# The squared deviations of four subsets: summed on GpSimd, and one averaging product behind the even image's first product

## The chip, the cores and the metric

The kernel runs on one core of a Trainium2 chip. The metric is the device time of the whole kernel in microseconds (us). Several engines work side by side: TensorE (PE) multiplies matrices, VectorE (DVE), ScalarE (ACT) and GpSimd (POOL) work elementwise, and 16 DMA engines move data between memory and the core's SBUF. SyncE (SP) only issues transfers here. The engines meet at semaphores.

## The reference, cut to what matters

```python
x = x + conv_block(group_norm(x, groups=32))          # x: (32, 512, 28, 28) float32

# group_norm: (x - mean) / sqrt(var + 1e-5) over 16 channels x 784 pixels of an image
# conv_block(v):
xg = v.reshape(B, 4, 128, H, W)[:, [1, 2, 3, 0]]      # groups rotated by one
xa = round(clip((xg - lA) / (uA - lA), 0, 1) * 15) / 15
wq = (round(clip((weight - lW) / (uW - lW), 0, 1) * 15) / 15 - 0.5) * 2
y  = einsum('bgihw,goi->bgohw', xa, wq.reshape(4, 128, 128))
y  = relu(y * inv + (beta - running_mean * inv))      # inv = gamma / sqrt(running_var + 1e-5)
return y + v
```

An image has 512 channels x 784 pixels in float32, 1.606 MB (1568 KB). All 32 are read once and written once.

## The kernel before, in words

**Tiling.** An image is four groups of 128 channels (one channel a partition) by 784 pixels. Images stand in a ring of `RING` = 12 buffers in SBUF. SyncE's queue loads image n whole; from n = 12 on it first waits until image n - 12 has been stored from the same buffer. ScalarE's queue stores images 0 to 29 whole, each once VectorE has finished its four groups; image 30 (L203) and the four groups of image 31, one by one (L212), are stored from SyncE's queue.

**Statistics, two images (a pair u) at a time.** For groups 0 and 1 VectorE takes means and squared deviations of four subsets of each channel's pixels (L460) and sums them over the subsets (`sum_stats`, L468); for groups 2 and 3 ScalarE takes the channel's mean (L236) and squared deviations from it (L242). Pairs 0 and 1 have three groups on VectorE. TensorE averages over the 16 channels of a norm group with a constant matrix: `average_means` gives the group means (L575, L576) and the first part of the variance (L578, which begins the sum in `var_ps`). ScalarE copies the means to SBUF (`gmean`, L250). GpSimd's `deviations` subtracts them from the subset means (L375) or channel means (L378), 2 images x 4 groups x 4 subsets, and squares the 32 values a channel (L382). `average_deviations` (L584) adds them to `var_ps` with one product for each of the four subsets. The variance then goes on: ScalarE makes half the variance and the standard deviation (L256, L257), VectorE the reciprocal (`rough_rstd`, L492), GpSimd a Newton step and the coefficients of two affine maps (`coefficients`, L398 to L406, each link waiting for the one before).

**The work on an image.** ScalarE (L270) and, for one group, GpSimd (L424) turn the input into levels; VectorE caps all four groups at once to bf16 codes (`cap`, L475). TensorE multiplies them by the weight, which is split in three bf16 parts: six matmuls of 392 columns a group (`multiply`, L604). Meanwhile GpSimd writes the affine part x + normalised x over the input (`affine`, L413; for the last four images ScalarE takes two of the groups, L278). TensorE waits for that affine before the last matmul of a group's product, so that VectorE's `finish` (L482), which adds the larger of product and floor to the image, needs only one semaphore.

**Order.** Each engine runs a list written out by hand. In round n GpSimd runs the affines of image n + 1 and its part of the levels of n + 2; before an odd n + 1 it makes the coefficients of the next pair, and in an even n + 1, behind the first affine, the `deviations` of pair (n + 3) // 2. VectorE runs finish 0 and 1 of image n, the cap of image n + 1, finish 2 and 3, the statistics of image n + 5 between and behind them, and for odd n the reciprocal at the end of the round. ScalarE runs levels, the stores, the sums of image n + 5, `deviation` (half variance and standard deviation) and the squares. TensorE runs the four products of image n + 1; for odd n `average_deviations` stands in front of the first, for even n `average_means` in front of the fourth. Three product buffers in PSUM (`SETS` = 3) stand between TensorE and VectorE. For pairs 0 and 1 the averages stand before and behind the very first product, an order of its own.

Of the kernel before, what the change touches and what calls it, by code (L numbers as in the profile page):

```python
# [5 lines left out]
ALU = mybir.AluOpType  # L6
ACT = mybir.ActivationFunctionType
AXIS = mybir.AxisListType
F32 = mybir.dt.float32
# [3 lines left out]
P = 128  # L13
# [13 lines left out]
SUBSETS = 4  # L27
# [3 lines left out]
def fused_norm_quantised_conv(nc, x, weight, limits, channel_params, out):  # L31

    B, C, H, W = x.shape
    G = CONV_GROUPS
# [11 lines left out]
    def stats_on_dve(u):  # L46
        return 3 if u < 2 else 2
# [6 lines left out]
    def affine_on_act(n):  # L54
        return 2 if n >= B - HELPED else 0
# [13 lines left out]
    def squares_until(u):  # L69
        return sum(2 * (G - stats_on_dve(i)) for i in range(u + 1))  # L70
# [7 lines left out]
    def output_group(g):  # L78
        return (g + G - 1) % G

    with ExitStack() as ctx:
        def sb(name, shape, dtype):
            return ctx.enter_context(nc.sbuf_tensor(name, shape, dtype))

        def ps(name, shape, dtype):
            return ctx.enter_context(nc.psum_tensor(name, shape, dtype))

        def sem(name):
            return ctx.enter_context(nc.semaphore(name))
# [8 lines left out]
        unused = sb("unused", [P, 2, HW], BF16)  # L98
        gmean = sb("gmean", [P, 2, 2, G], F32)
        dev = sb("dev", [P, 2, G, SUBSETS], F32)  # L100
        dev2 = sb("dev2", [P, 2, G, SUBSETS], F32)
        half_var = sb("half_var", [P, 2 * G], F32)
        std = sb("std", [P, 2, G], F32)
        rough = sb("rough", [P, 2, G], F32)
# [26 lines left out]
        avg = sb("avg", [P, P], F32)  # L131
# [5 lines left out]
        var_ps = ps("var_ps", [P, 512], F32)  # L137
# [26 lines left out]
        dev_step = sem("dev_step")  # L164
        dev_done = sem("dev_done")
        var_done = sem("var_done")
# [162 lines left out]
        def _(pool):  # L329
            step = [0]  # L330

            def chained(ins):
# [33 lines left out]
                                    cols[:, 1].unsqueeze(1).to_broadcast([P, 2, G]),  # L366
                                    bn[:, 4].unsqueeze(1).to_broadcast([P, 2, G]), ALU.subtract)

            def deviations(u):
                k, par = stats_on_dve(u), u % 2  # L370
                pool.wait_ge(gmean_done, u + 1)
                if u >= 1:
                    pool.wait_ge(var_done, u)
                mean = gmean[:, par].unsqueeze(3)
                nc.gpsimd.tensor_tensor(dev[:, :, 0:k], stats[:, par, :, 0:k, :, 1],  # L375
                                        mean[:, :, 0:k].to_broadcast([P, 2, k, SUBSETS]), ALU.subtract)
                own = sums[:, par, 0].unsqueeze(3)
                nc.gpsimd.tensor_tensor(dev[:, :, k:G], own[:, :, k:G].to_broadcast([P, 2, G - k, SUBSETS]),  # L378
                                        mean[:, :, k:G].to_broadcast([P, 2, G - k, SUBSETS]),
                                        ALU.subtract).then_inc(dev_step, 1)  # L380
                pool.wait_ge(dev_step, u + 1)
                nc.gpsimd.tensor_tensor(dev2[:], dev[:], dev[:], ALU.mult).then_inc(dev_done, 1)  # L382

            LINKS = 6

# [172 lines left out]
        @block.tensor  # L558
        def _(pe):
            pe.wait_ge(consts_done, 1)  # L560
            pe.wait_ge(rows_in, DMA)
            nc.tensor.transpose(cols_ps[:, 0:4 * G], rows[:], ident[0:4 * G, 0:4 * G])
            pe.wait_ge(limits_in, DMA)
            nc.tensor.matmul(cols_ps[:, 4 * G:5 * G], one_row[:], limit_row[:], start=True,
                             stop=True).then_inc(cols_turned, 1)

            def average_means(u):
                k, par = stats_on_dve(u), u % 2
                pe.wait_ge(bn_summed, u + 1)
                pe.wait_ge(squared, squares_until(u))  # L570
                if u >= 1:
                    pe.wait_ge(gmean_done, u)
                    pe.wait_ge(std_done, u)
                mean = mean_ps[:, 0:2 * G].rearrange("p (j g) -> p j g", g=G)
                nc.tensor.matmul(mean[:, :, 0:k], avg[:], sums[:, par, 0, :, 0:k], start=True, stop=True)  # L575
                nc.tensor.matmul(mean[:, :, k:G], avg_one[:], sums[:, par, 0, :, k:G], start=True,  # L576
                                 stop=True).then_inc(mean_done, 1)
                nc.tensor.matmul(var_ps[:, 0:2 * G], avg_n[:], sums[:, par, 1], start=True, stop=False)  # L578

            def average_deviations(u):  # L580
                pe.wait_ge(dev_done, u + 1)
                var = var_ps[:, 0:2 * G].rearrange("p (j g) -> p j g", g=G)
                for s in range(SUBSETS):
                    done = nc.tensor.matmul(var, avg[:], dev2[:, :, :, s], start=False, stop=(s == SUBSETS - 1))  # L584
                done.then_inc(var_done, 1)


            def wait_affine(n, g):
                if g < G - affine_on_act(n):
                    pe.wait_ge(y_pool, (y_pool_until(n - 1) if n else 0) + g + 1)  # L590
                else:
                    pe.wait_ge(y_act, y_act_until(n - 1) + g - (G - affine_on_act(n)) + 1)

            def multiply(n, g):
                k = G * n + g
                if g == 0:
                    pe.wait_ge(capped, n + 1)
                if k >= SETS:
                    pe.wait_ge(final, k - SETS + 1)
                for part in range(PARTS):  # L600
                    for h in range(2):
                        if (part, h) == (PARTS - 1, 1):
                            wait_affine(n, g)
                        done = nc.tensor.matmul(prod[:, k % SETS, h, 0:HALF], w_t[:, part, output_group(g)],  # L604
                                                codes[:, n % 2, g, h * HALF:(h + 1) * HALF],
                                                start=(part == 0), stop=(part == PARTS - 1))
                done.then_inc(multiplied, 1)

            pe.wait_ge(w_scaled, 1)
            for g in range(G):  # L610
                turned = nc.tensor.transpose(prep_ps[:, g], w_raw[:, g], ident[:])
            turned.then_inc(w_turned, 1)
            average_means(0)
            average_deviations(0)
            pe.wait_ge(w_ready, 1)

            for n in range(-1, B - 1):
                if n < 0:
                    average_means(1)
                    multiply(0, 0)  # L620
                    average_deviations(1)
                    multiply(0, 1)
                    multiply(0, 2)
                else:
                    if n % 2 and (n + 3) // 2 < PAIRS:
                        average_deviations((n + 3) // 2)
                    multiply(n + 1, 0)
                    multiply(n + 1, 1)
                    multiply(n + 1, 2)
                    if n % 2 == 0 and (n + 4) // 2 < PAIRS:  # L630
                        average_means((n + 4) // 2)
                multiply(n + 1, 3)
# [23 lines left out]
```

## Time and profile before

| | before |
|---|---|
| median of 3 runs | 258.73 us (258.67 to 258.85) |
| profiled execution, its own time | 258.41 us |
| its span, first to last instruction | 256.7 us |
| mean granted TensorE clock | 0.902 of full speed |
| TensorE busy | 193.9 us (76%) |
| VectorE busy | 230.0 us (90%) |
| ScalarE busy | 215.2 us (84%) |
| GpSimd busy | 212.0 us (83%) |
| moved | 103.25 MB, mean 402 GB/s |

The profile is of one execution. "Span" leaves out what lies before the first and behind the last instruction, 1.7 us here. Busy shares are averages over the whole span; in the middle of it VectorE, ScalarE and GpSimd are each busy over nine tenths of the time. In the rows below a name such as L604 is a line of the kernel. "a<-b" is output and inputs, x6 the number of instructions merged in a row, and a bracket at the end the idle time in front of it with what ended it. The row of lengths of a merged group runs from its first start to its last end.

### The profile page before, as it was taken

What the parts mean: (1) busy time and instruction counts of PE and PEld (TensorE: products, weight loads), DVE (VectorE), ACT (ScalarE), POOL (GpSimd) and SP (SyncE); (2) the same over time, 40 slices, a digit from 0 to 9 for tenths busy, and PEclk for the clock granted to TensorE, in tenths of its full rate; (3) what the DMA queues carried; (4) which work ended last, traced back from release to release, by engine and by line L of the source; (5) the groups of instructions that cost most, each with busy time, mean ns of one, the idle gap of its engine ahead of it and who ended that gap; (6) DMA issues with size and microseconds to landing.
All of it is one profiled execution on the core that took longest, in us unless ns stands there. A gap on an engine that the chain in (4) does not pass through costs nothing.

```text
span 256.7 us, 3463 instructions
## 1 busy us (share of the span) xinstructions
PE 193.9 (76%) x999; PEld 109.3 (43%) x999; DVE 230.0 (90%) x363; ACT 215.2 (84%) x394; POOL 212.0 (83%) x340
## 2 busy tenths in 40 slices
PE   1142996969889888979797997877696969889920
PEld 0132644435454444445443554343444435454510
DVE  2898698999999999999999899999999999969940
ACT  4437898999999999989999889999899888999300
POOL 6126869999999999999999999999999999999100
PEclk9999999797979798988979599999979797979995
DMA  6999999999999999999999999999999999999994
GB/s 225 398 411 411 408 409 406 418 416 417 418 414 418 417 416 418 411 418 416 416 415 416 418 416 413 419 417 415 417 413 418 416 418 409 402 400 402 393 399 193
DMA packets 34516, 103.25 MB, mean 402 GB/s; under 512 B 1202, under 2 KB 1730, under 8 KB 34498
## 3 DMA queue, kind: packets, MB, share of 16 engines
q1 hardware_dynamic: 18624, 54.86, 53.8%
q10 hardware_dynamic: 15874, 48.18, 47.0%
q8 instruction: 8, 0.13, 0.2%
q14 instruction: 10, 0.08, 0.1%
HBM read 51.65 MB, written 51.38 MB: 401 GB/s over the span
## 4 chain that ended last, share of the span: by engine, by line
POOL 52%; DVE 16%; issue 11%; PE 9%; ACT 5%; DMA 2%; DVEq 0%; SPq 0%; POOLq 0%; ACTq 0%
POOL images L413 27%; POOL levels L424 8%; DVE images L482 7%; PE prod L604 6%; DVE stats L460 4%; POOL dev L375 3%; DVE codes L475 3%; PE var_ps L584 3%; POOL dev L378 2%; DMA images<-in_x 2%; POOL scaled L404 2%; ACT levels L270 2%; POOL coef L406 2%; POOL norm L402 1%; ACT unused L242 1%
## 5 line engine op out<-in xcount | busy, mean ns | idle before, releaser
L604 PE MATMUL prod<-codes,w_t 128*128 128x392 bf16 x768 | 160.8, 369 | 7.9 <-DVE codes L475 2.9
L482 DVE SCALAR_TENSOR_TENSOR images<-prod,floor,images 128x784 f32<-128x784 f32 x128 | 128.0, 1019 | 8.5 <-PE prod L604 8.2
L413 POOL TENSOR_SCALAR images<-images,coef 128x784 f32<-128x784 f32 x120 | 123.7, 1042 | 0.0
L604 PEld LDWEIGHTS prod<-codes,w_t 128*128 128x128 bf16 x768 | 79.1, 110 | 81.6 <-issue 24.6
L270 ACT ACTIVATE levels<-images,coef 128x784 int16<-128x784 f32 x95 | 91.3, 1028 | 1.1 <-issue 1.1
L460 DVE BATCH_NORM_STATS2 stats<-images 128x6 f32<-128x392 f32 x136 | 68.9, 551 | 5.4 <-DMA images<-in_x 5.4
L236 ACT ACTIVATE unused<-images 128x784 bf16<-128x784 f32 x60 | 50.7, 847 | 7.5 <-DMA images<-in_x 5.2
L242 ACT ACTIVATE unused<-images,sums 128x784 bf16<-128x784 f32 x60 | 56.1, 939 | 0.1
L475 DVE TENSOR_SCALAR codes<-levels 128x3136 bf16<-128x3136 int16 x32 | 34.7, 1085 | 1.0 <-ACT levels L270 0.7
L584 PE MATMUL var_ps<-dev,avg 128*128 128x8 f32 x128 | 19.6, 280 | 20.0 <-POOL dev L382 20.0
L424 POOL TENSOR_SCALAR levels<-images,coef 128x784 int16<-128x784 f32 x33 | 33.6, 1020 | 0.1
L584 PEld LDWEIGHTS var_ps<-dev,avg 128*128 128x128 f32 x128 | 18.6, 221 | 25.4 <-POOL dev L382 25.2
L375 POOL TENSOR_TENSOR dev<-stats,gmean 128x16 f32<-128x16 f32 (+1 forms) x16 | 10.9, 682 | 9.6 <-ACT gmean L250 9.6
L575 PE MATMUL mean_ps<-sums,avg 128*128 128x4 f32 (+1 forms) x32 | 6.5, 274 | 12.2 <-DVE sums L468 12.2
L575 PEld LDWEIGHTS mean_ps<-sums,avg 128*128 128x128 f32 x32 | 5.2, 203 | 17.2 <-DVE sums L468 12.2
L242 ACT ACTIVATION_READ_ACCUMULATOR unused<-images,sums 128x1 f32 x60 | 11.4, 190 | 0.0
L236 ACT ACTIVATION_READ_ACCUMULATOR unused<-images 128x1 f32 x60 | 11.3, 188 | 0.0
L256 ACT ACTIVATE half_var<-var_ps,eps 128x8 f32<-128x8 f32 x16 | 4.2, 265 | 6.7 <-PE var_ps L584 6.4
L398 POOL TENSOR_TENSOR newt<-rough 128x8 f32<-128x8 f32 x16 | 3.9, 242 | 5.5 <-DVE rough L492 5.5
L250 ACT ACTIVATE gmean<-mean_ps 128x8 f32<-128x8 f32 x16 | 2.7, 170 | 6.1 <-PE mean_ps L576 6.0
L278 ACT ACTIVATE images<-images,coef 128x784 f32<-128x784 f32 x8 | 7.7, 1032 | 0.0
L404 POOL TENSOR_TENSOR scaled<-norm,coef_mul 128x32 f32<-128x32 f32 x16 | 6.5, 409 | 1.2
(66 smaller groups left out, 83.2 us busy)
## 6 DMA issues: line engine op xcount, KB each, us to landing
images<-in_x SPq DMA_DIRECT2D x30, 1568.0 KB, 14.5
out<-images ACTq DMA_DIRECT2D x30, 1568.0 KB, 18.8
images<-in_x SPq DMA_DIRECT2D x8, 392.0 KB, 6.6
out<-images SPq DMA_DIRECT2D x1, 1568.0 KB, 8.8
out<-images SPq DMA_DIRECT2D x4, 392.0 KB, 7.4
w_raw<-in_weight SPq DMA_DIRECT2D x1, 256.0 KB, 6.5
rows<-in_channel_params ACTq DMA_DIRECT2D x1, 8.0 KB, 2.3
limit_row<-in_limits ACTq DMA_DIRECT2D x1, 0.0 KB
```

The source lines that it names most:

```text
L236: nc.scalar.activation(unused[:, g % 2], images[:, n % RING, g], ACT.Identity, scale=1.0 / HW, accum_out=sums[:, u % 2, 0, j, g:g + 1]).th ...
L242: nc.scalar.activation(unused[:, g % 2], images[:, n % RING, g], ACT.Square, scale=-1.0, bias=sums[:, u % 2, 0, j, g:g + 1], accum_out=sum ...
L270: nc.scalar.activation(levels[:, n % 2, g], images[:, n % RING, g], ACT.Relu, bias=coef[:, u % 2, 1, 0, G * j + g:G * j + g + 1], scale=co ...
L375: nc.gpsimd.tensor_tensor(dev[:, :, 0:k], stats[:, par, :, 0:k, :, 1], mean[:, :, 0:k].to_broadcast([P, 2, k, SUBSETS]), ALU.subtract)
L413: nc.gpsimd.tensor_scalar(here, here, coef[:, u % 2, 0, 1, G * j + o:G * j + o + 1], coef[:, u % 2, 1, 1, G * j + o:G * j + o + 1], ALU.mu ...
L424: nc.gpsimd.tensor_scalar(levels[:, n % 2, g], images[:, n % RING, g], coef[:, u % 2, 0, 0, G * j + g:G * j + g + 1], coef[:, u % 2, 1, 0, ...
L460: nc.vector.bn_stats(two, images[:, n % RING, g, h * HALF:(h + 1) * HALF]).then_inc(bn_done, 1)
L475: nc.vector.tensor_scalar(codes[:, n % 2], levels[:, n % 2], 0.0, TOP, ALU.max, ALU.min).then_inc(capped, 1)
L482: nc.vector.scalar_tensor_tensor(out=two, in0=prod[:, k % SETS, :, 0:HALF], scalar=floor[:, o:o + 1], in1=two, op0=ALU.max, op1=ALU.add).t ...
L575: nc.tensor.matmul(mean[:, :, 0:k], avg[:], sums[:, par, 0, :, 0:k], start=True, stop=True)
L584: done = nc.tensor.matmul(var, avg[:], dev2[:, :, :, s], start=False, stop=(s == SUBSETS - 1))
L604: done = nc.tensor.matmul(prod[:, k % SETS, h, 0:HALF], w_t[:, part, output_group(g)], codes[:, n % 2, g, h * HALF:(h + 1) * HALF], start= ...
```

## The change

GpSimd no longer stops at the 32 squares a channel. It adds the four subsets in two steps, 16 additions and then 8, so that 8 values (2 images x 4 groups) are left. Each of the two steps that read what the one before wrote waits for its semaphore. TensorE averages these 8 with one product instead of four. And in the rounds with odd n this product stands behind the first product of the even image n + 1 instead of in front of it. The order for pairs 0 and 1 stays.

```diff
-        dev2 = sb("dev2", [P, 2, G, SUBSETS], F32)
+        dev2 = sb("dev2", [P, 2 * G, SUBSETS], F32)
+        dev2_half = sb("dev2_half", [P, 2 * G, SUBSETS // 2], F32)
+        dev2_sum = sb("dev2_sum", [P, 2 * G], F32)
...
+            FOLDS = 3
+
+            def folded(u, k, ins):
+                ins.then_inc(dev_step, 1)
+                pool.wait_ge(dev_step, FOLDS * u + k)
+
             def deviations(u):
...
-                nc.gpsimd.tensor_tensor(dev[:, :, k:G], own[:, :, k:G].to_broadcast([P, 2, G - k, SUBSETS]),
-                                        mean[:, :, k:G].to_broadcast([P, 2, G - k, SUBSETS]),
-                                        ALU.subtract).then_inc(dev_step, 1)
-                pool.wait_ge(dev_step, u + 1)
-                nc.gpsimd.tensor_tensor(dev2[:], dev[:], dev[:], ALU.mult).then_inc(dev_done, 1)
+                folded(u, 1, nc.gpsimd.tensor_tensor(dev[:, :, k:G], own[:, :, k:G].to_broadcast([P, 2, G - k, SUBSETS]),
+                                                     mean[:, :, k:G].to_broadcast([P, 2, G - k, SUBSETS]), ALU.subtract))
+                dev_ = dev[:].rearrange("p j g s -> p (j g) s")
+                folded(u, 2, nc.gpsimd.tensor_tensor(dev2[:], dev_, dev_, ALU.mult))
+                folded(u, 3, nc.gpsimd.tensor_tensor(dev2_half[:], dev2[:, :, 0:2], dev2[:, :, 2:4], ALU.add))
+                nc.gpsimd.tensor_tensor(dev2_sum[:], dev2_half[:, :, 0], dev2_half[:, :, 1], ALU.add).then_inc(dev_done, 1)
...
             def average_deviations(u):
                 pe.wait_ge(dev_done, u + 1)
-                var = var_ps[:, 0:2 * G].rearrange("p (j g) -> p j g", g=G)
-                for s in range(SUBSETS):
-                    done = nc.tensor.matmul(var, avg[:], dev2[:, :, :, s], start=False, stop=(s == SUBSETS - 1))
-                done.then_inc(var_done, 1)
+                nc.tensor.matmul(var_ps[:, 0:2 * G], avg[:], dev2_sum[:], start=False, stop=True).then_inc(var_done, 1)
...
                 else:
+                    multiply(n + 1, 0)
                     if n % 2 and (n + 3) // 2 < PAIRS:
                         average_deviations((n + 3) // 2)
-                    multiply(n + 1, 0)
                     multiply(n + 1, 1)
```

## Rows read from the trace of the kernel before

**Rows 1.** The page: DMA share and GB/s in 40 slices; the chain by engine.
```profile
DMA  6999999999999999999999999999999999999994
...
GB/s 225 398 411 411 408 409 406 418 416 417 418 414 418 417 416 418 411 418 416 416 415 416 418 416 413 419 417 415 417 413 418 416 418 409 402 400 402 393 399 193
...
POOL 52%; DVE 16%; issue 11%; PE 9%; ACT 5%; DMA 2%; DVEq 0%; SPq 0%; POOLq 0%; ACTq 0%
```

**Rows 2.** Busy time by windows: window, length, engines, PEclk, DMA share, GB/s.
```profile
235.00:240.00 5.00, 4.50 (x28) 2.43 (x26) 5.00 (x6) 4.89 (x6) 3.48 (x3) 1.00 1.04 403
...
250.00:255.00 5.00, 0.00 (x0) 0.00 (x0) 0.00 (x0) 0.00 (x0) 0.00 (x0) 0.55 0.68 266
...
255.00:256.00 1.00, 0.00 (x0) 0.00 (x0) 0.00 (x0) 0.00 (x0) 0.00 (x0) 0.50 0.02 9
```

**Rows 3.** Timeline around the deviations of one pair: start, length, engine, line.
```profile
110.96 1.17 PE L604 MATMUL prod<-codes,w_t 128*128 128x392 bf16 x6
...
111.76 0.97 DVE L475 TENSOR_SCALAR codes<-levels 128x3136 bf16<-128x3136 int16 x1
...
111.82 0.99 POOL L378 TENSOR_TENSOR dev<-sums,gmean 128x16 f32<-128x16 f32 x1
...
112.89 0.24 POOL L382 TENSOR_TENSOR dev<-dev 128x32 f32<-128x32 f32 x1
...
113.11 2.96 POOL L413 TENSOR_SCALAR images<-images,coef 128x784 f32<-128x784 f32 x3
...
113.18 1.21 PE L584 MATMUL var_ps<-dev,avg 128*128 128x8 f32 x8 [1.05 <-POOL dev L382]
...
114.59 0.26 ACT L257 ACTIVATE std<-var_ps,eps 128x8 f32<-128x8 f32 x1
...
116.42 0.18 DVE L492 RECIPROCAL rough<-std 128x8 f32<-128x8 f32 x1
...
117.01 0.20 POOL L398 TENSOR_TENSOR newt<-rough 128x8 f32<-128x8 f32 x1
...
117.29 0.21 POOL L399 TENSOR_TENSOR newt<-newt,half_var 128x8 f32<-128x8 f32 x1
```

**Rows 4.** Timeline: the squarings of pairs 2 and 15.
```profile
43.42 0.24 POOL L382 TENSOR_TENSOR dev<-dev 128x32 f32<-128x32 f32 x1
...
225.04 0.24 POOL L382 TENSOR_TENSOR dev<-dev 128x32 f32<-128x32 f32 x1
```

**Rows 5.** Timeline of the end: VectorE and the issues of stores.
```profile
228.10 1.03 DVE L482 SCALAR_TENSOR_TENSOR images<-prod,floor,images 128x784 f32<-128x784 f32 x1 [1.01 <-PE prod L604]
...
230.06 1.03 DVE L482 SCALAR_TENSOR_TENSOR images<-prod,floor,images 128x784 f32<-128x784 f32 x1 [0.93 <-PE prod L604]
...
238.55 0.38 ACTq L262 DMA_DIRECT2D out<-images  x1
...
241.20 5.73 DVE L482 SCALAR_TENSOR_TENSOR images<-prod,floor,images 128x784 f32<-128x784 f32 x6
...
243.19 0.39 SPq L203 DMA_DIRECT2D out<-images  x1
```

**Rows 6.** Chain that ended last, in order of time: start, length, what.
```profile
0.79 0.38 SPq L191
...
1.70 5.61 DMA images<-in_x
```

**Rows 7.** Timeline of the start.
```profile
22.84 0.19 ACT L242 ACTIVATION_READ_ACCUMULATOR unused<-images,sums 128x1 f32 x1
...
26.86 2.14 PE L604 MATMUL prod<-codes,w_t 128*128 128x392 bf16 x6 [0.55 <-DVE codes L475]
...
28.79 1.71 PE L584 MATMUL var_ps<-dev,avg 128*128 128x8 f32 x8
...
30.54 0.27 ACT L256 ACTIVATE half_var<-var_ps,eps 128x8 f32<-128x8 f32 x1 [0.91 <-PE var_ps L584]
```

**Rows 8.** Who waited for whom: total us, times, longest.
```profile
POOL newt L398 <- DVE rough L492: 5.5, 3, 2.8
```

## The prediction, made before the kernel was changed

> **What bounds the kernel now.** I read the page's slices first. The DMA row stands at 9 from the second slice to the last but one [rows 1]: the 103 MB of loads and stores keep all 16 DMA engines occupied from about 5 us on, so that a compute engine that gets faster has nothing to give by itself. The GB/s row shows three stretches: about 410 while only loads run (to about 40 us), about 416 while loads and stores mix, about 401 when only stores are left (from about 215 us). The second look is at the last 20 us. At 235 to 240 us the engines are full at 403 GB/s; from 250 us on, 266 GB/s x 5 us = 1.33 MB are still moved, and the last traffic lies between 255 and 256 us [rows 2]. At 401 GB/s those 1.33 MB would be done at 253.3 us: this is the mean engine's end. The last of the 16 ends near 255.5 us. The difference, 2.2 us, is skew between the engines.
>
> The third view is the chain of waits: 52% of the chain that ended last is GpSimd [rows 1]. In the timeline of a pair of images GpSimd's instructions follow each other with no wait in front of them [rows 3], and the squaring of the deviations comes at 43.42 us for pair 2 and at 225.04 us for pair 15 [rows 4]: 181.6 us for 13 pairs, 13.97 us a pair. For a pair the DMA engines move four images of 1.606 MB (two in, two out), 15.4 us at 416 GB/s. So there are two clocks. Compute, paced by GpSimd, is the faster one by 1.5 us a pair, and the difference stands in a backlog of stores, until about 215 us. From there only stores are left, 4.0 us each at 401 GB/s, while compute delivers one each 7 us and at the end one each 4.65 us (238.55 and 243.19 us, [rows 5]): the backlog is eaten. When image 30's store is issued at 243.19 us, images 30 and 31 still need 2 x 1.606 / 0.401 = 8.0 us. The mean engine has 253.3 - 243.2 = 10.1 us to go, so its backlog ahead of them is 2.1 us; the last engine's is 255.5 - 243.2 - 8.0 = 4.3 us. A new store takes time before it moves data: the first load is issued at 0.79 and the transfer that the chain follows begins at 1.70 us [rows 6], 0.9 us. So compute may end later by 2.1 - 0.9 = 1.2 us before the mean engine runs dry ahead of image 30, and by 4.3 - 0.9 = 3.4 us before the last one does. That slack is what the change must be measured against.
>
> **The change part by part.**
>
> *Two adds more on GpSimd, in each of 16 pairs.* Now the squaring (0.24 us) is followed at once by the next affine, 113.11 - 112.89 = 0.22 us after its start [rows 3]. Afterwards: a link of the coefficients, 0.20 us of work, is followed by the next after 117.29 - 117.01 = 0.28 us, so its wait adds 0.08 [rows 3]. The squaring with such a wait is 0.24 + 0.08 = 0.32 us; the add of 16 elements with one 0.28 us (the link has 8); the last add, 0.20 us. Together 0.80, less 0.22: 0.58 us a pair. From below, an add could cost only its 0.20 us, 0.40 together; from above, L378 with 16 elements took 0.99 us where VectorE's 4x-rate cap of 3136 elements ran beside it (111.76 to 112.73 us, [rows 3]), some 0.77 us more than alone. But GpSimd, never idle, meets each of the two caps of a pair already; a third meeting would need a third cap. I take 0.58. Nothing hides it, since GpSimd waits for nobody: pairs 2 to 14 add 13 x 0.58 = 7.5 us by the time that pair 15 is reached. Behind the adds in GpSimd's queue stand three affines of the even image (TensorE's last matmul of each product waits for them), then its part of the quantising (the cap waits for it), then the next pair's coefficients.
>
> *Six TensorE instructions less a pair* (three fp32 matmuls, each seen twice, with their loads). The eight take 1.21 us in [rows 3], so some 0.9 us goes; with them goes the 1.05 us in which TensorE stood before the squares. TensorE is not what paces the pairs, so this is worth nothing in the steady state; it cancels part of the delay elsewhere.
>
> *The averaging product behind the first product.* The first product starts when its cap is done (112.73 us) and needs 1.17 us at the high clock, as that at 110.96 us, to about 113.95. The sum of squares is ready at 112.89 + 0.80 = 113.7. So the averaging product runs from about 113.95 to 114.35, where the eight instructions now end at 113.18 + 1.21 = 114.39 [rows 3]. The variance arrives when it did, though 0.58 us of it was added: ScalarE and VectorE see no new delay. At the low clock the product takes about 2.1 us (the first one, 26.86 us, [rows 7]) and the variance comes up to 0.9 us later; the standard deviation, done at 114.85 us, lies for 1.57 us before VectorE's reciprocal takes it at 116.42 us [rows 3], which covers it.
>
> *The start.* For pairs 0 and 1 the old order stays, and TensorE's burst is on the path. For pair 1 the eight take 1.71 us and ScalarE waits 0.91 us for them [rows 7]; GpSimd stands idle for the reciprocal behind the second product [rows 8]. Two instructions instead of eight give back 1.2 us there; the 0.58 us of GpSimd lies in its wait. For pair 0 ScalarE's own statistics end when the coefficients do, so only about 0.2 us comes through (22.84 us, [rows 7]). Gain: 1.4 us, once.
>
> *The few waits that GpSimd does have.* It waits for the reciprocal three times, 5.5 us in all, 2.8 us the longest [rows 8]; all but 0.3 us of that is in pairs 0 and 1. Another 0.2 us or so stands before the means. A later GpSimd doesn't wait: 0.5 us back.
>
> *The end.* In pair 15 TensorE sets the pace once: VectorE waits 1.01 and 0.93 us for products 0 and 1 of image 28 [rows 5], because the averaging stands in front of both. With product 0 ahead of it I give back 1.4 us of these 1.94 (between 0.9 and 1.9).
>
> *The sum.* Compute ends later by 7.5 - 1.4 - 0.5 - 1.4 = 4.2 us: VectorE's last write moves from 246.9 [rows 5] to 251.1, and image 30's store from 243.2 to 247.4. The slack for the last engine is 3.4 us: 0.8 us is left over. By the mean engine (slack 1.2) it would be 3.0. Since the end is that of the last of the 16, I go near the lower: +1.0 us. The profiled execution took 258.41 us, span 256.7; it becomes 259.4 with span 257.7. The median of the runs is 0.3 us above it: 258.73 + 1.0 = 259.7.
>
> The Trainium skill ("DMA: Bandwidth & Descriptors", on the anatomy of one DMA) puts a fixed cost of about 2 us on each DMA, most of it the receipt of the write. Such a receipt counts at the very end, where it stands now too, so that the sum is the same; were all 2 us in front of the data, the time would be 1.1 us above my figure. The trace shows 0.9 us in front at the first load and, behind the last traffic, about 1 us to the end of the span.
>
> **Rivals.**
>
> *Hidden.* The time stays within 258.2 to 259.2. This needs compute to end no more than 3.9 us later, for instance with adds at 0.5 us a pair (13 x 0.08 = 1.0 us less) or an end that gives back all 1.9. The DMA row at 9 throughout speaks for it; against it, the deliveries at the end have a margin that the sum uses up. Place of the forecast within this: 258.9.
>
> *Faster.* The 16 engines share what memory gives; if the ones that run dry leave their share to the slow ones, the skew of 2.2 us goes. Image 30's store then ends at 243.2 + d + 0.9 + 8.0 = 252.1 + d against 255.5, with d the delay of compute, but not before the mean's 253.3. It is faster by over 0.5 us for d under 2.9. With d = 2.4 this gives -1.0 us, 257.7. That d is under 2.9 needs GpSimd's addition to be 0.48 us a pair or less, and the skew has survived all of the run so far. Little speaks for it. The earlier first store (0.9 us at 416 instead of 410 GB/s) is worth 0.01 us.
>
> *Much slower.* GpSimd loses more than its two adds (a cap that fell across an affine and now holds two small ones, or VectorE held up by GpSimd's quantising, which it follows closely): 0.8 us a pair, d = 7.1, 3.7 us left over for the last engine: 262.4.
>
> **How the numbers follow.** What this kernel's runs can tell from no change is about 0.2%, 0.5 us. Forecast (slower by 0.5 to 3 us, likeliest 259.7): 0.57. Hidden: 0.28. Faster: 0.08. Much slower: 0.07. Slower is 0.57 + 0.07 = 0.64. The range takes in the hidden case down to 258.3 and goes up to the mean-engine bound, 258.73 + 3.0, cut a little: 261.5. It leaves out the faster and the much slower case and some of each edge, about 0.18.
>
> **What would show each step right or wrong.** The distance of the squarings of pairs 2 and 15, 181.6 us now, should be 189 us (187 to 190); if it stays under 184, the adds don't pace the pairs. The L413 behind the last add should begin 0.80 us after the squaring. The averaging should be two instructions a pair with no wait on GpSimd of more than 0.3 us, and end as early after the squaring as before. VectorE's last write should come at about 251 us, image 30's store at 247.4. The DMA row should show its first gap behind 235 us, where there is none now: 1 us windows below 0.9 between 238 and 250. If compute ends 4 us later and the span is the same, the skew gave it back; if compute doesn't end later, GpSimd wasn't the pace.

## The result, and the profile of the changed kernel

| | before | changed |
|---|---|---|
| median, 6 runs each | 258.70 us (258.44 to 258.93) | 259.88 us (259.35 to 260.25) |
| ratio | | 1.0041, 95% interval 1.0026 to 1.0057 |
| span of the profiled execution | 256.7 us | 257.8 us |
| TensorE busy | 193.9 us | 169.0 us |
| GpSimd busy | 212.0 us | 219.5 us |

The kernel became slower by 0.4%, 1.1 to 1.2 us; forecast was 259.7 us with a span of 257.7. TensorE is busy 25 us less and the kernel is later all the same. Of the 25 us, 13.0 are the averaging products (19.6 us before, 6.6 after) and 6.4 the image products, which are as many as before and run at a higher mean granted clock (0.947, before 0.902).

The page of the changed kernel, the same slices and chain as in [rows 1]:

```profile
DMA  6999999999999999999999999999999999998798
...
GB/s 214 396 411 411 409 406 414 415 418 416 418 418 414 418 416 418 416 412 417 418 417 418 414 417 417 417 419 413 414 418 418 417 413 411 402 389 332 315 363 324
...
POOL 70%; issue 9%; DVE 6%; DMA 6%; SPq 2%; ACT 2%; PE 2%; DVEq 0%; POOLq 0%; ACTq 0%
```

GpSimd's share of the chain rose from 52% to 70%. The GB/s row is nearly the old one as far as slice 35 and falls to 332 and 315 in slices 37 and 38, where the kernel before kept 402 and 393: the transfers run short of work near the end. In windows of 1 us (same columns as [rows 2]; the share of the DMA engines is the last number but one):

```profile
232.00:233.00 1.00, 1.00 (x6) 0.77 (x5) 0.32 (x1) 0.15 (x1) 1.00 (x2) 0.50 0.83 323
...
233.00:234.00 1.00, 1.00 (x5) 0.47 (x4) 0.69 (x2) 1.00 (x3) 0.86 (x3) 0.50 0.54 210
...
238.00:239.00 1.00, 1.00 (x8) 0.53 (x6) 1.00 (x2) 1.00 (x2) 1.00 (x2) 1.00 0.17 66
...
243.00:244.00 1.00, 1.00 (x8) 0.62 (x7) 1.00 (x2) 1.00 (x2) 1.00 (x2) 1.00 0.33 126
...
248.00:249.00 1.00, 1.00 (x8) 0.59 (x7) 1.00 (x2) 0.00 (x0) 0.00 (x0) 1.00 0.45 182
...
255.00:256.00 1.00, 0.00 (x0) 0.00 (x0) 0.00 (x0) 0.00 (x0) 0.00 (x0) 0.50 1.03 408
...
256.00:257.00 1.00, 0.00 (x0) 0.00 (x0) 0.00 (x0) 0.00 (x0) 0.00 (x0) 0.50 0.48 185
```

At 233 to 234 us the engines are 0.54 busy, at 238 to 239 only 0.17, at 243 to 244 0.33, at 248 to 249 0.45. Each gap lies in front of the data of one more image. The first clear one, at 232 to 234 us, is in front of image 27, whose store is issued at 232.86 us (before at 226.63). Behind the last gap they stay full until 256 us and stop within 1 us, whereas before the traffic ebbed away over 3 us:

```profile
252.00:253.00 1.00, 0.00 (x0) 0.00 (x0) 0.00 (x0) 0.00 (x0) 0.00 (x0) 0.50 0.79 304
253.00:254.00 1.00, 0.00 (x0) 0.00 (x0) 0.00 (x0) 0.00 (x0) 0.00 (x0) 0.50 0.43 166
254.00:255.00 1.00, 0.00 (x0) 0.00 (x0) 0.00 (x0) 0.00 (x0) 0.00 (x0) 0.50 0.14 53
```

One pair in the timeline, against [rows 3]:

```profile
111.84 0.99 POOL L422 TENSOR_SCALAR images<-images,coef 128x784 f32<-128x784 f32 x1
...
111.97 1.75 DVE L484 TENSOR_SCALAR codes<-levels 128x3136 bf16<-128x3136 int16 x1 [0.32 <-ACT levels L272]
...
113.77 1.17 PE L610 MATMUL prod<-codes,w_t 128*128 128x392 bf16 x6 [1.78 <-DVE codes L484]
...
114.05 0.24 POOL L389 TENSOR_TENSOR dev<-dev 128x32 f32<-128x32 f32 x1
...
114.36 0.21 POOL L390 TENSOR_TENSOR dev_half<-dev 128x16 f32<-128x16 f32 x1
...
114.66 0.20 POOL L391 TENSOR_TENSOR dev_sum<-dev_half 128x8 f32<-128x8 f32 x1
...
114.84 2.94 POOL L422 TENSOR_SCALAR images<-images,coef 128x784 f32<-128x784 f32 x3
...
114.91 0.39 PE L591 MATMUL var_ps<-dev_sum,avg 128*128 128x8 f32 x2
...
115.50 0.26 ACT L259 ACTIVATE std<-var_ps,eps 128x8 f32<-128x8 f32 x1
...
117.40 0.18 DVE L501 RECIPROCAL rough<-std 128x8 f32<-128x8 f32 x1
...
119.29 1.08 POOL L409 TENSOR_TENSOR newt<-three_halves,newt 128x8 f32<-128x8 f32 x1
...
119.34 0.96 DVE L484 TENSOR_SCALAR codes<-levels 128x3136 bf16<-128x3136 int16 x1
```

The affine behind the adds starts 0.79 us after the squaring (114.84 - 114.05), where it was 0.22. TensorE's first product (113.77) now stands in front of the averaging, which is two instructions of 0.39 us and is over at 115.30, 1.25 us behind the start of the squaring; it was 1.50 before. (Where the first product falls in a stretch of the low clock the averaging comes later. In the next pair the product takes 2.14 us at half the clock and ScalarE waits 1.67 us for the averaging; in all it waits 11.1 us, 6.4 before.) ScalarE's standard deviation is done at 115.76 and VectorE takes it at 117.40: 1.6 us of cover, as before.

The squarings of pairs 2 and 15, against [rows 4]:

```profile
41.07 0.24 POOL L389 TENSOR_TENSOR dev<-dev 128x32 f32<-128x32 f32 x1
...
230.77 0.24 POOL L389 TENSOR_TENSOR dev<-dev 128x32 f32<-128x32 f32 x1
```

189.7 us for 13 pairs, 14.59 us a pair, against 13.97. The pairs are alike here, 14.58 to 14.60 us each; before, most took 13.8 to 14.0 and one took 15.1.

The end, against [rows 5]; what stands in front of image 30's store decides:

```profile
230.50 2.09 PE L610 MATMUL prod<-codes,w_t 128*128 128x392 bf16 x6 [1.75 <-DVE codes L484]
...
233.31 0.20 DVE L501 RECIPROCAL rough<-std 128x8 f32<-128x8 f32 x1 [0.98 <-ACT std L259]
...
238.34 0.38 ACTq L264 DMA_DIRECT2D out<-images  x1
...
242.99 0.38 ACTq L264 DMA_DIRECT2D out<-images  x1
...
245.64 5.73 DVE L491 SCALAR_TENSOR_TENSOR images<-prod,floor,images 128x784 f32<-128x784 f32 x6
...
247.63 0.39 SPq L205 DMA_DIRECT2D out<-images  x1
```

VectorE ends at 251.4 us (before 246.9), and image 30's store is issued at 247.63 us (before 243.19): compute is 4.4 us later.

Who waited for whom:

```profile
PE prod L610 <- DVE codes L484: 30.1, 31, 1.8
...
PE prod L610 <- POOL images L422: 17.7, 14, 1.5
...
POOL newt L407 <- DVE rough L501: 1.5, 1, 1.5
```

TensorE's products now wait 30.1 us for the caps and 17.7 us for GpSimd's affines, 2.9 and 1.2 us before; its wait for the squares went the other way, from 20.0 to 2.0 us. It is the engine with time to spare. GpSimd waits for the reciprocal only once, 1.5 us in pair 0.

### The profile page after: what moved, and what is told of

The parts are those of the page before. It is cut to its first block, busy times and chain, and to the rows that moved or that the text cites. A ratio compares the mean times of both kernels' runs of the same rounds, so it can differ in the third digit from the quotient of the medians.

```text
span 257.8 us, 3303 instructions
## 1 busy us (share of the span) xinstructions
PE 169.0 (66%) x903; PEld 89.2 (35%) x903; DVE 236.9 (92%) x363; ACT 215.0 (83%) x394; POOL 219.5 (85%) x372
## 4 chain that ended last, share of the span: by engine, by line
POOL 70%; issue 9%; DVE 6%; DMA 6%; SPq 2%; ACT 2%; PE 2%; DVEq 0%; POOLq 0%; ACTq 0%
POOL images L422 37%; POOL levels L433 11%; DMA images<-in_x 6%; POOL newt L409 6%; POOL dev L383 5%; DVE images L491 4%; DVE codes L484 2%; SPq L193 2%; PE prod L610 1%; POOL newt L408 1%; POOL coef L415 1%; POOL dev L389 1%; POOL scaled L413 1%; POOL dev_half L390 1%; POOL norm L410 1%
## 5 line engine op out<-in xcount | busy, mean ns | idle before, releaser
L610 PE MATMUL prod<-codes,w_t 128*128 128x392 bf16 x768 | 154.4, 350 | 60.2 <-DVE codes L484 30.1
L422 POOL TENSOR_SCALAR images<-images,coef 128x784 f32<-128x784 f32 x120 | 119.5, 1007 | 0.0
L610 PEld LDWEIGHTS prod<-codes,w_t 128*128 128x128 bf16 x768 | 72.9, 106 | 133.0 <-DVE codes L484 42.4
L484 DVE TENSOR_SCALAR codes<-levels 128x3136 bf16<-128x3136 int16 x32 | 42.0, 1311 | 5.7 <-POOL levels L433 3.4
L383 POOL TENSOR_TENSOR dev<-stats,gmean 128x16 f32<-128x16 f32 (+1 forms) x16 | 14.6, 910 | 10.0 <-ACT gmean L252 10.0
L409 POOL TENSOR_TENSOR newt<-three_halves,newt 128x8 f32<-128x8 f32 x16 | 14.6, 915 | 1.3
L258 ACT ACTIVATE half_var<-var_ps,eps 128x8 f32<-128x8 f32 x16 | 4.2, 262 | 11.1 <-PE var_ps L591 11.1
L591 PEld LDWEIGHTS var_ps<-dev_sum,avg 128*128 128x128 f32 x32 | 6.4, 233 | 6.8 <-POOL dev_sum L391 6.1
L591 PE MATMUL var_ps<-dev_sum,avg 128*128 128x8 f32 x32 | 6.6, 279 | 2.0 <-POOL dev_sum L391 2.0
L587 PE MATMUL var_ps<-sums,avg_n 128*128 128x8 f32 x32 | 6.3, 269 | 0.0
```

What stands on the lines that cost most here:

```text
L409: linked(u, 3, nc.gpsimd.tensor_tensor(newt[:, 2], three_halves[:], newt[:, 1], ALU.subtract))
L422: nc.gpsimd.tensor_scalar(here, here, coef[:, u % 2, 0, 1, G * j + o:G * j + o + 1], coef[:, u % 2, 1, 1, G * j + o:G * j + o + 1], ALU.mu ...
L484: nc.vector.tensor_scalar(codes[:, n % 2], levels[:, n % 2], 0.0, TOP, ALU.max, ALU.min).then_inc(capped, 1)
L591: nc.tensor.matmul(var_ps[:, 0:2 * G], avg[:], dev2_sum[:], start=False, stop=True).then_inc(var_done, 1)
```

## The experiments

Between pairs 2 and 15 lie 13 pair lengths. Each kernel was timed beside the kernel before on the same chip. The before row is that of the first series; the kernel before had medians of 258.87, 258.31 and 258.80 us in the others, and the ratios go by these. The table gathers what the profiles show of each kernel that stores image 30 whole: the distance of the squarings of pairs 2 and 15, the issue of image 30's store (S30), and the span.

| kernel | 13 pairs, us | S30, us | span, us | median, us | ratio to before (95%) |
|---|---|---|---|---|---|
| before | 181.6 | 243.2 | 256.7 | 258.70 | |
| order only | 183.1 | 243.0 | 257.6 | 258.71 | 0.9999 (0.9982 to 1.0017) |
| one add | 185.9 | 244.8 | 257.1 | 258.45 | 0.9985 (0.9969 to 1.0002) |
| late end, 6 instructions | 182.5 | 247.5 | 258.1 | 259.74 | 1.0041 (1.0019 to 1.0063) |
| changed | 189.7 | 247.6 | 257.8 | 259.88 | 1.0041 (1.0026 to 1.0057) |
| adds only | 188.4 | 248.1 | 258.2 | 259.89 | 1.0044 (1.0030 to 1.0059) |
| idle adds | 188.6 | 250.9 | 261.4 | 264.97 | 1.0235 (1.0195 to 1.0274) |
| late end, 12 instructions | 182.7 | 251.0 | 261.1 | 263.02 | 1.0173 (1.0145 to 1.0201) |
| four adds | 194.5 | 253.5 | 263.6 | 265.38 | 1.0263 (1.0239 to 1.0287) |

**The order alone.**

```diff
                 else:
+                    multiply(n + 1, 0)
                     if n % 2 and (n + 3) // 2 < PAIRS:
                         average_deviations((n + 3) // 2)
-                    multiply(n + 1, 0)
```

> The kernel before with one part of the change alone: the four averaging products stand behind the first product of the even image; GpSimd adds nothing. My theory (GpSimd paces the pairs, transfers set the end): the distance from the squaring of pair 2 to that of pair 15 stays at 181.6 us (within 1), VectorE ends at or before 246.9 us, the DMA row shows no gap, and the time is that of before, 258.7 us within 0.3. Rival (the order is what costs, because the variance comes later): the pairs get longer than 14.2 us and the time goes above 259.2.

Measured: 258.71 us, ratio 0.9999. The timeline of its end:

```profile
226.44 0.24 POOL L382 TENSOR_TENSOR dev<-dev 128x32 f32<-128x32 f32 x1
...
240.96 5.73 DVE L482 SCALAR_TENSOR_TENSOR images<-prod,floor,images 128x784 f32<-128x784 f32 x6
...
242.95 0.39 SPq L203 DMA_DIRECT2D out<-images  x1
```

The pair distance is 183.1 us, 1.5 longer than before and half a microsecond outside what I had written. Two kernels below whose pairs are untouched show 182.5 and 182.7, but by other means: they have two pairs of 15.1 us among pairs of 13.4 to 14.1, where the kernel before has one. Here ten of the 13 pairs take 14.03 us, within 0.05. So the new order seems to cost some 0.1 us a pair; "adds only" against the changed kernel says the same below. One of the small links of the coefficients now meets the second cap of a pair (L402 takes 0.76 us on average, 0.26 before). From the squaring of pair 15 to VectorE's end it takes 20.25 us instead of 21.9: the new order gives 1.6 us back at the end. Cost and gain cancel, and the time shows neither.

**The adds without the order**: the changed kernel with the two lines of the order as they were.

> The changed kernel with the old order: the two adds and the one averaging product are kept, but the product stands in front of the first product of the even image. My theory: the pairs take 14.6 us as in the changed kernel, and the end gives back less, since TensorE stands before the sum once more: VectorE ends between 251.4 and 253 us and the time is 259.9 to 261.3, likeliest 260.5. Rival (the order is what costs): 258.7, as before.

Measured: 259.89 us, ratio 1.0044, at the lower edge of the expected range.

```profile
229.42 0.24 POOL L389 TENSOR_TENSOR dev<-dev 128x32 f32<-128x32 f32 x1
...
246.12 5.73 DVE L491 SCALAR_TENSOR_TENSOR images<-prod,floor,images 128x784 f32<-128x784 f32 x6
...
248.11 0.39 SPq L205 DMA_DIRECT2D out<-images  x1
```

The whole loss is there without the order. 188.4 us for 13 pairs is 14.49 a pair, 1.3 us less in all than with the new order, and the end takes 22.4 us from the squaring, 1.8 more than in the changed kernel, as it should with TensorE standing before the sum again.

**One add instead of two**, and two products for the two halves.

```diff
-            FOLDS = 3
+            FOLDS = 2
...
-                folded(u, 3, nc.gpsimd.tensor_tensor(dev2_half[:], dev2[:, :, 0:2], dev2[:, :, 2:4], ALU.add))
-                nc.gpsimd.tensor_tensor(dev2_sum[:], dev2_half[:, :, 0], dev2_half[:, :, 1], ALU.add).then_inc(dev_done, 1)
+                nc.gpsimd.tensor_tensor(dev2_half[:], dev2[:, :, 0:2], dev2[:, :, 2:4], ALU.add).then_inc(dev_done, 1)
...
-                nc.tensor.matmul(var_ps[:, 0:2 * G], avg[:], dev2_sum[:], start=False, stop=True).then_inc(var_done, 1)
+                for s in range(2):
+                    done = nc.tensor.matmul(var_ps[:, 0:2 * G], avg[:], dev2_half[:, :, s], start=False, stop=(s == 1))
+                done.then_inc(var_done, 1)
```

> The changed kernel with only the first of the two adds, and two averaging products for the two halves. Theory: 0.3 us a pair less on GpSimd, so 14.3 us a pair, compute ends 13 x 0.3 = 3.9 us earlier than in the changed kernel, at 247.5 us, within the slack of 3.4 us behind the kernel before: 258.7 us, the same as before, with at most shallow gaps in the DMA row. Rival (cost in proportion to the adds, no slack): half of the loss, 259.3.

Measured: 258.45 us, ratio 0.9985 with an interval that holds 1. The rival's 259.3 (1.002) lies outside it.

```profile
228.42 0.24 POOL L388 TENSOR_TENSOR dev<-dev 128x32 f32<-128x32 f32 x1
...
242.82 5.73 DVE L489 SCALAR_TENSOR_TENSOR images<-prod,floor,images 128x784 f32<-128x784 f32 x6
...
244.81 0.39 SPq L204 DMA_DIRECT2D out<-images  x1
```

14.30 us a pair, as written; VectorE ends at 248.5 us where I had written 247.5. Compute is 1.6 us later than before, which is inside the slack: no loss. Short gaps are there (DMA share 0.78 at 240 to 241 us, 0.74 at 245 to 246), and behind them the traffic still ebbs away as before (0.78, 0.13 and 0.06 from 253 us on). The second add is the one that is paid for, though both take the same time.

**Four adds**: the changed kernel with two links more into a spare tile.

```diff
-            FOLDS = 3
+            FOLDS = 5
...
+                for k in range(2):
+                    folded(u, 4 + k, nc.gpsimd.tensor_tensor(spare[:, k], dev2_half[:, :, 0], dev2_half[:, :, 1], ALU.add))
                 nc.gpsimd.tensor_tensor(dev2_sum[:], dev2_half[:, :, 0], dev2_half[:, :, 1], ALU.add).then_inc(dev_done, 1)
```

> The changed kernel with two adds more in the same chain, into a spare tile that nobody reads (0.29 us each with the wait). Theory: 15.15 us a pair, compute ends 13 x 0.57 = 7.4 us later than in the changed kernel, at 258.8 us, and since the slack is used up all of it shows: 259.9 + 7.4 = 267.3 us (266.5 to 268). Rival (cost in proportion to the adds): 1.2 us more, 261.1.

Measured: 265.38 us, 5.5 us above the changed kernel. The rival (1.2 us more) is out; past the slack a delay shows in full, S30 5.9 us later and span 5.8 us longer. My figure was 1.9 us too high and its range (from 266.5) missed, mainly because a pair grew by 0.37 us and not by 0.57. Most of the other 0.2 us is in its timeline:

```profile
121.96 0.98 DVE L487 TENSOR_SCALAR codes<-levels 128x3136 bf16<-128x3136 int16 x1
...
122.10 0.90 POOL L411 TENSOR_TENSOR newt<-newt,half_var 128x8 f32<-128x8 f32 x1
```

The second link of the coefficients lasts 0.90 us beside the cap. In the changed kernel the third link did, for 1.08 us (119.29 and 119.34 us above). The link is held until the cap ends, so what a cap costs GpSimd depends on how the two starts fall: 0.70 us beyond the link's own 0.20 here, where the link begins 0.14 us behind the cap, 0.88 there, where it begins just ahead of it. Over all 16 pairs the three links take 19.4 us here and 21.8 in the changed kernel, 0.15 us a pair. A pair's length is the sum of GpSimd's work plus such remainders, and adding work moves them.

**Idle adds**: the kernel before, four products and the old order, with two adds into a spare tile in front of the squaring.

```diff
-                pool.wait_ge(dev_step, u + 1)
+                pool.wait_ge(dev_step, 3 * u + 1)
+                for k in range(2):
+                    nc.gpsimd.tensor_tensor(spare[:, k], dev[:, 0, :, 0:2], dev[:, 1, :, 0:2], ALU.add).then_inc(dev_step, 1)
+                    pool.wait_ge(dev_step, 3 * u + 2 + k)
                 nc.gpsimd.tensor_tensor(dev2[:], dev[:], dev[:], ALU.mult).then_inc(dev_done, 1)
```

> The kernel before (four averaging products, old order) with two small adds in GpSimd's chain in front of the squaring, into a spare tile that nobody reads. It shows GpSimd's side of the change without the fewer products. Theory: 14.55 us a pair, the start keeps its four products and gives nothing back, so the squaring of pair 2 stays near 43.4 us and VectorE ends near 253.8 us; slack 3.4 us, so 3.5 us more than before: 262.2 us (261 to 263). Rival (fewer products are worth nothing at either end, being hidden): 259.9, as with the adds alone.

Measured: 264.97 us, from 263.0 to 266.2; the profiled execution is one of the short ones, 263.13 us with a span of 261.4.

```profile
233.03 0.86 POOL L386 TENSOR_TENSOR dev<-dev 128x32 f32<-128x32 f32 x1
...
248.88 5.73 DVE L486 SCALAR_TENSOR_TENSOR images<-prod,floor,images 128x784 f32<-128x784 f32 x6
...
250.88 0.39 SPq L204 DMA_DIRECT2D out<-images  x1
```

Its squaring of pair 2 comes at 44.40 us. The pair is 14.51 us long on average, so GpSimd's two instructions alone make the slower pace, whatever they add. (The single pairs differ, 13.96 to 15.17 us.) VectorE's caps take no longer than before (33.9 us in all, 34.7 before, 42.0 in the changed kernel), so it isn't they that make it. Against "adds only" it is 3.2 us slower in the profiled executions (263.13 and 259.98 us) and 5.1 by the medians: that is about what the fewer products are worth once the slack is gone. In the profiles the difference lies before pair 2 (44.40 against 41.04 us). My 262.2 us was too low by 0.9 us against the profiled execution, since compute came 7.7 us later and not 6.9, and by 2.8 against the median, which is outside my range; what makes its other executions up to 3 us longer isn't in the profile and stays open.

**A later end with the pace untouched**: the kernel before, with statistics instructions on VectorE whose result nobody uses, in front of the cap of image 29; six in one kernel, twelve in the other.

```diff
+                if n == 28:
+                    for k in range(6):
+                        nc.vector.bn_stats(spare[:, k], w_rest[:].rearrange("p g o -> p (g o)")[:, 0:HALF])
                 if n + 1 < B:
                     cap(n + 1)
```

> The kernel before with six statistics instructions more on VectorE (0.48 us each, result unused) in front of the cap of image 29: compute ends 2.9 us later, the pace of the pairs is untouched. Theory (slack of 3.4 us, up to the last of the 16 engines): VectorE ends at 249.8 us, short gaps in the DMA row behind 240 us, and the time is unchanged, 258.7 within 0.5. Rival (slack of only 1.2 us, up to the mean engine): 260.4.

> The same with twelve instructions: compute ends 5.8 us later, at 252.7 us. Theory: 5.8 - 3.4 = 2.4 us more, 261.1 us (260.6 to 261.8), by the issue of image 30's store (249.0) + 0.9 + 8.0 = 257.9 us for the last traffic. Rival (slack of 1.2 us): 263.3. Rival (loss in proportion to the delay, no slack): 264.5.

With six, 259.74 us was measured where I had written 258.7:

```profile
231.55 1.03 DVE L483 SCALAR_TENSOR_TENSOR images<-prod,floor,images 128x784 f32<-128x784 f32 x1 [0.93 <-PE prod L608]
...
232.50 2.90 DVE L546 BATCH_NORM_STATS2 spare<-w_rest 128x6 f32<-128x392 f32 x6
...
245.50 5.73 DVE L483 SCALAR_TENSOR_TENSOR images<-prod,floor,images 128x784 f32<-128x784 f32 x6
...
247.49 0.39 SPq L204 DMA_DIRECT2D out<-images  x1
```

The six take 2.8 us (232.50 to 235.32), as intended, but this execution reached them 1.5 us late (its product at 231.55, 230.06 in [rows 5]), so VectorE ends at 251.2: a delay of 4.3 us, almost that of the changed kernel, and with the same ratio, 1.0041. The run didn't test the inside of the slack, which "one add" does; it shows that 4.3 us of delay cost the same 0.4% when they come from VectorE at the end as when they come from GpSimd pair by pair. With twelve, 263.02 us, outside my range of 260.6 to 261.8:

```profile
248.99 5.74 DVE L483 SCALAR_TENSOR_TENSOR images<-prod,floor,images 128x784 f32<-128x784 f32 x6
...
250.98 0.39 SPq L204 DMA_DIRECT2D out<-images  x1
```

The delay is 7.8 us instead of the 5.8 I had meant: this execution, too, reached the instructions late, by 1.2 us, and lost the rest behind them. So the rival's 263.3, though near, had the wrong delay. The loss is 4.2 us, against 7.8 - 3.4 = 4.4 by the last engine's slack and 6.6 by the mean engine's.

**Group stores**: images 28 to 30 stored group by group, as image 31 is; once on the changed kernel, once on the kernel before.

```diff
-ACT_STORES = 30
+ACT_STORES = 28
...
-            for n in range(ACT_STORES, B - 1):
-                store(n)
-            for g in range(G):
-                o = output_group(g)
-                sync.wait_ge(final, G * (B - 1) + g + 1)
-                sync.dma_start(out_v[B - 1][:, o], images[:, (B - 1) % RING, o]).then_inc(stored[(B - 1) % RING], DMA)
+            for n in range(ACT_STORES, B):
+                for g in range(G):
+                    o = output_group(g)
+                    sync.wait_ge(final, G * n + g + 1)
+                    sync.dma_start(out_v[n][:, o], images[:, n % RING, o]).then_inc(stored[n % RING], DMA)
```

> The changed kernel, with images 28 to 30 stored group by group from SyncE's queue as image 31 is, so that three quarters of an image can leave up to 3 us earlier. Compute is unchanged. Theory (the loss is the gaps in the DMA row between 237 and 249 us, while a store waits for the fourth group): these gaps close for the most part, VectorE still ends near 251.4 us, and the time comes back by 0.5 to 1.5 us, to 258.4 to 259.4, likeliest 258.9. Rival (the late end of VectorE itself sets the time, or the adds slow the transfers): no change, 259.9.

> The same group stores in the kernel before, as a control. Theory: its DMA row has no gap at the end, so there is nothing to close: 258.7 us within 0.4, possibly slightly more for the extra issues. Rival (group stores help by themselves): faster by 0.5 us or more.

Measured: on the changed kernel 258.36 us beside 258.31 us of the kernel before (ratio 1.0009, 1.0000 to 1.0019). The changed kernel wasn't timed in the same series, but by the ratios the 0.41% shrinks to 0.09%; on the 258.70 us of the first series that makes the 258.9 I had written. On the kernel before 258.61 beside 258.31 (1.0012, 1.0002 to 1.0022): nothing to gain there, and about 0.1% to lose. With group stores in both, the changed kernel is no slower. The page of the former:

```profile
DMA  6999999999999999999999999999999999999995
...
GB/s 232 395 412 409 409 406 417 412 417 417 418 417 414 418 416 417 415 413 417 417 417 417 414 417 416 418 420 411 414 418 417 417 414 414 403 397 373 390 402 226
```

The slices that had 332, 315 and 363 GB/s have 373, 390 and 402. VectorE still ends late, at 250.6 us:

```profile
244.91 5.74 DVE L490 SCALAR_TENSOR_TENSOR images<-prod,floor,images 128x784 f32<-128x784 f32 x6
```

This execution's compute is 0.7 us earlier than that of the changed kernel (it started so; its 13 pairs take 189.7 us too), and with whole images it would by the model below lose 0.3 us instead of 1.0. So the profile alone doesn't carry the verdict. Two things do: the gaps at 238, 243 and 248 us are not there (the one in front of image 27, which is stored whole, still is, 0.64 at 232 to 233 us), though image 31 is still being computed until 250.6; and the ratio is that of 11 runs. The late end of compute by itself is not what costs; the gaps in front of whole images are.

**One add and group stores together**, the version with the least compute delay and no gaps.

> One add, two averaging products, and the group stores for images 28 to 30: the version with the shortest compute delay and no gaps. Theory: the transfers set the time, so this is the same as before, 258.2 to 258.9; it can't be faster than before by more than 0.3 us. Rival (the single add version was truly 0.15% faster and the gaps cost something too): 258.0 or less beside a kernel before of 258.7.

Measured: 258.75 us, ratio 0.9999 (0.9983 to 1.0015). As written: nothing is to be had beyond the transfers. No kernel tried beats the one before by more than the measurement tells.

## Why the prediction was right

**GpSimd sets the pairs.** Forecast 0.58 us more a pair and 189 us for 13 pairs, measured 0.62 and 189.7. "Idle adds" shows it with sums that nobody reads, "adds only" without the new order. That GpSimd would meet no third cap held: in the pair shown, one small instruction in front of the squaring (L383, 0.99 us from 112.80) and one link are held; before it was L378 (0.99 us, [rows 3]) and an affine. What I had as a fixed price of the meetings isn't one: it moves by 0.2 us with where the cap falls, as "four adds" shows.

**The averaging behind the first product.** The variance was to come as soon after the squaring as before; in the pair shown it came 0.25 us earlier. I had put the order's effect on the pairs at nothing. It is 1.3 us over 13 pairs beside the adds (189.7 against 188.4) and 1.5 without them (183.1 against 181.6); the end gives as much back, and "order only" shows the sum to be free. So the costly part of the change is not the one on TensorE.

**The start.** Given back were 2.35 us (43.42 to 41.07 us), where I had 1.4. The term was undersized, though the mechanism is that of the fewer products: "idle adds", with four products, has no such gain (44.40 us).

**The few waits of GpSimd** (0.5 us back) can't be told apart from the pace: 13 pairs grew by 8.1 us, against 7.5 - 0.5 = 7.0 written. The adds by themselves brought 6.8 ("adds only") and 7.0 ("idle adds"), near what was written; the rest is the order.

**The end.** 1.3 us given back, 1.4 written (from the squaring of pair 15 to VectorE's last write: 21.9 us before, 20.6 after). The sum: 8.1 - 2.35 - 1.3 = 4.4 us, written 4.2. The errors of the start and of the pace, 0.95 and 1.1 us, cancelled. That part of the agreement is luck.

**The slack.** This is the step that turned 4.4 us into 1.1. Span = S30 + 0.9 + 8.0 and about 1.2 us for the end was the model; the six kernels with S30 at 247.5 us or later have spans of S30 + 10.1 to S30 + 10.6, and the three with S30 up to 244.8 us lie at 256.7 to 257.6, independent of it. The knee, 256.7 - 10.1 = 246.6 us, is 3.4 us behind the store of before. It is where two lines meet: no run lies between 244.8 and 247.5 us, each point is one execution, and the executions of the kernel before differ by up to 2 us in span, so that the slack is known to about 1 us. The mean engine's slack of 1.2 us, the upper bound, is not what counts: delays of 1.6, 4.4, 4.9 and 7.8 us ("one add", changed, "adds only", twelve instructions) cost nothing, 1.1, 1.0 and 4.2 us, where it gives 0.4, 3.2, 3.7 and 6.6. "Four adds" (10.3 us) lost 6.5, against 9.1. Only "idle adds" (7.7 us) fits neither well, with 4.7 lost in its profiled execution and 6.2 by the median, against 4.3 by the last engine and 6.5 by the mean.

**The first gap** was to come between 238 and 250 us and came at 232. The backlog was eaten one image earlier than I had worked out, since image 27 came 6.2 us late. The time doesn't depend on it: five images from 232.86 + 0.9 us on would end at 253.8, two from 247.63 + 0.9 on end at 256.5.

**The rivals.** *Hidden* fell with the delay, 4.4 us and not under 3.9. *Faster* needed a delay under 2.9 us; the skew did go (full until 256 us, over within 1 us). But that doesn't show that the engines that run dry leave their share to the slow ones: past the last engine's slack all 16 would have run dry and begin on image 30 together, which looks the same. No view here shows single engines. "One add" had the delay for it, 1.6 us, which by that rival gives 252.1 + 1.6 = 253.7 instead of 255.5, 1.8 us less; measured was 0.15% less, 0.4 us, not clear of zero, and the traffic ebbed away as before. That speaks against the sharing. *Much slower* needed 0.8 us a pair.

## What to carry to other kernels

A kernel whose transfers are busy throughout still has a compute path with a slack of its own: find where the backlog of transfers is eaten, and measure the change in the pace of the pacing engine against that slack, not against busy shares. Work taken from an engine with time to spare and given to the engine that nothing makes wait is paid for once a pair, even in instructions of 0.2 us; here 7.5 us more of GpSimd's time stand against 25 us less of TensorE's, and the kernel lost. When the last results come so late that gaps open in front of the last transfers, store them in smaller pieces; where there are no gaps it gains nothing.

## What the runs showed of the hardware that was not expected

A small GpSimd instruction that meets VectorE's cap (int16 to bf16, 3136 elements) doesn't slow down in proportion but is held until the cap ends: L409 with 8 elements, 0.20 us alone, began at 119.29 us and ended at 120.37, 0.07 us behind the cap. It works the other way too. The cap that begins at 111.97 us, while GpSimd is in an affine until 112.83, takes 1.75 us instead of 0.97. The Trainium skill ("GPSIMD Engine Reference", key points) says that GpSimd shares its SBUF interfaces with VectorE and contends with instructions in a two-port mode; the trace shows such contention between GpSimd and the cap, though no view names the cap's mode, and it shows the one waiting for the other's end.

The ebbing of the traffic at the end, which I read as 2.2 us of skew between the 16 DMA engines, was gone after four gaps that add up to about 3 us, and was still there after the two gaps of 0.2 to 0.3 us in "one add".

The mean granted clock of TensorE rose from 0.902 to 0.947 while its busy share fell from 76% to 66%. It goes with the order of the instructions and not with the share: "order only" and "adds only" both have 71%, and their clocks are 0.942 and 0.881. In this kernel the clock was worth nothing: the changed kernel and "adds only" take the same time, 259.88 and 259.89 us, at 0.947 and 0.881.
